# Attention and quantised feed-forward on one core: other units for VectorE, down weights turned in their own tile, eight row buffers and biases spread by a product

## The reference

```python
xn = layernorm(x)                                   # over 1024, no affine
# attention: for each row, its 32 heads attend to each other (D = 32)
q, k, v = (xn @ Wq.T + bq), (xn @ Wk.T + bk), (xn @ Wv.T + bv)     # -> (B, S, 32, 32)
s = einsum('bshd,bsgd->bshg', q, k) / sqrt(32)
s = where(s > 0.001, s, -inf)
o = einsum('bshg,bsgd->bshd', softmax(s), v).reshape(B, S, 1024)
attn = o @ Wo.T + bo
# feed-forward, inner width 3584
Wg, Wu, Wd = dequant(gate_q, gate_s), dequant(up_q, up_s), dequant(down_q, down_s)
ffn = (silu(xn @ Wg.T) * (xn @ Wu.T)) @ Wd.T
out = x + attn + ffn
```

## Time and profile before

| | |
|---|---|
| median of 3 runs | 2102.8 us (2102.1 to 2103.78) |
| the profiled execution | 2104.22 us, span from first to last instruction 2102.2 us |
| opening, to the first scores | 0 to 79.5 us |
| attention and output projection | to about 857 us |
| feed-forward tiles 0 and 1, few or no downs yet | to 935 us |
| feed-forward tiles 2 to 26 | 935 to 2005 us |
| tile 27 | 2005 to 2047 us |
| tail | 2047 to 2102.2 us |
| TensorE, VectorE, ScalarE, GpSimd busy | 96%, 76%, 60%, 64% |

### The profile page before, as it was taken

One profiled execution on the slowest core, in us unless ns is written; L12 is line 12 of the kernel. 1 busy time (PEld: TensorE's weight loads), 2 busy tenths in 40 slices (PEclk: granted clock), 3 DMA queues, 4 the chain that ended last, 5 costly groups with the idle time before them and its releaser, 6 DMA issues. The chain is left out here.

```text
span 2102.2 us, 36938 instructions
## 1 busy us (share of the span) xinstructions
PE 2017.6 (96%) x10880; PEld 972.4 (46%) x10880; DVE 1592.0 (76%) x1584; ACT 1252.8 (60%) x2017; POOL 1349.7 (64%) x769
## 2 busy tenths in 40 slices
PE   7899999999998899899999999999999999999997
PEld 5555555555554444334444444444444444444444
DVE  5666766667665300599899989999899989998996
ACT  4578778777775311255666566665656566656653
POOL 1445554645543000058888888888888888888886
PEclk9999999999999999999999999999999999999999
DMA  8363553554454352122122212222112212221208
GB/s 290 91 132 88 106 133 85 113 121 90 111 109 130 101 195 97 30 70 61 45 50 70 60 45 50 53 63 59 48 46 70 60 45 50 68 55 51 50 22 324
DMA packets 330006, 185.97 MB, mean 88 GB/s; under 512 B 269168, under 2 KB 306032, under 8 KB 329968
## 3 DMA queue, kind: packets, MB, share of 16 engines
q1 hardware_dynamic: 329968, 185.46, 34.0%
HBM read 96.29 MB, written 25.17 MB: 58 GB/s over the span
## 5 line engine op out<-in xcount | busy, mean ns | idle before, releaser
L644 PE MATMUL banks<-xt,lower 128*128 128x512 f16 x3584 | 861.7, 379 | 30.0 <-ACT lower L895 16.3
L1212 POOL TENSOR_TENSOR acc<-acc,lower 128x1024 f32<-128x1024 f32 x327 | 772.8, 2368 | 175.2 <-ACT lower L922 175.2
L922 ACT ACTIVATE lower<-banks,down_scale 128x512 f32<-128x512 f32 x654 | 413.8, 683 | 355.9 <-PE banks L669 264.0
L1099 DVE SCALAR_TENSOR_TENSOR lower<-banks,gate_scale,lower 128x1024 f32<-128x1024 f32 x392 | 479.2, 1278 | 146.2 <-PE banks L644 140.2
L644 PEld LDWEIGHTS banks<-xt,lower 128*128 128x128 f16 x3584 | 337.4, 98 | 486.6 <-DVE lower L1099 80.2
L499 PE MATMUL banks<-wt,xt_tile 128*128 128x512 f16 x2304 | 540.0, 380 | 4.2 <-ACT wt L743 2.6
L1099 DVE SCALAR_TENSOR_TENSOR lower<-banks,up_scale,lower 128x1024 f32<-128x1024 f32 x392 | 479.5, 1278 | 51.1 <-PE banks L644 44.9
L669 PE MATMUL banks<-lower 128*128 (+1 forms) x1792 | 458.8, 380 | 5.0 <-DMA lower<-lower 4.4
L1174 POOL TENSOR_TENSOR stacks<-unit,stacks 128x512 f16<-128x512 f32 x192 | 246.7, 1308 | 286.6 <-ACT stacks L768 286.5
L499 PEld LDWEIGHTS banks<-wt,xt_tile 128*128 (+1 forms) x2304 | 215.8, 98 | 220.6 <-issue 4.7
L669 PEld LDWEIGHTS banks<-lower 128*128 (+1 forms) x1792 | 175.2, 98 | 217.6 <-issue 17.3
(11 more groups left out here) (57 smaller groups left out, 1305.8 us busy)
## 6 DMA issues: line engine op xcount, KB each, us to landing
lower<-in_L_ffn_gate_q_dram SPq DMA_DIRECT2D x28, 512.0 KB, 3.7
lower<-in_L_ffn_up_q_dram SPq DMA_DIRECT2D x28, 512.0 KB, 4.5
lower<-in_L_ffn_down_q_dram SPq DMA_DIRECT2D x28, 512.0 KB, 4.1
x_tile<-in_L_attn_x_dram SPq DMA_DIRECT2D x16, 512.0 KB, 3.8
xt_scratch<-xt_tile SPq DMA_DIRECT2D x16, 512.0 KB, 2.8
ctx_scratch<-ctx_parts SPq DMA_DIRECT2D x64, 128.0 KB, 2.1
lower<-ctx_scratch SPq DMA_DIRECT2D x4, 2048.0 KB, 9.2
xt<-xt_scratch SPq DMA_DIRECT2D x4, 2048.0 KB, 15.4
```

What stands on the lines that cost most here:

```text
L644: last = mm(psum[:, 2 * (slot % 3) + c, :], gu_t[:, mat, g, :], xt[:, (2 * half + c) * CT:(2 * half + c + 1) * CT, part, g, :], start=(par ...
L922: run(down_tmp[:, buffer, c * BANK:(c + 1) * BANK], psum[:, 6 + c, :], ACT.Copy, scale=scale)\
L1099: v.scalar_tensor_tensor(out=acc_of[:, half, :], in0=gu_pair(slot % 3), scalar=scale[:, :, :].rearrange("p t k -> p (t k)")[:, bass.ds(t * ...
L1212: g.tensor_tensor(acc[:, half, ho, :], acc[:, half, ho, :], down_tmp[:, buffer, :], ALU.add).then_inc(down_added, 1)
```

## The change

Feed-forward:

- The fast downs are `d` 0, 2, 8 and 10, at units 16, 20, 0 and 4 (`d % 8 in (0, 2)`); there are still 4 of 16.
- GpSimd's `hidden` for half 1 comes after unit 7 and no longer after unit 10. ScalarE's second SiLU comes at unit 27 and no longer at 23.
- The down weights of tile `t` are converted in tile `t` (after unit 25) and turned behind it, no longer in tile `t + 1`. Gate is converted after unit 9 (was 21), up after unit 29 (was 27).
- In the tail ScalarE's conversion of the last down weights is gone, and its two HI parts stand ahead of its second and fourth copies, no longer ahead of all copies.

Opening:

- `w_rows` holds eight blocks (`ROWS = 8`), so blocks are loaded up to eight ahead, and the quarters begin at `w = 8` (eight of them come after the last block).
- The three bias rows are loaded to one partition each. TensorE multiplies a column of ones with them (two float32 products of 512 columns for each row), and ScalarE copies the result to `bias_qkv`, ahead of everything but its first square root. The blocks `w` 1 and 2 wait for all three copies.
- The second row tile is normed in steps at `w` 10 to 13 and turned behind the load of block 21. `bo` is loaded last.

```diff
-                w_rows = sb(s1, "w_rows", [P, 4, H], F32)
+                w_rows = sb(s1, "w_rows", [P, ROWS, H], F32)
...
-            for w in range(4, 3 * KT):
-                weights(w)
-                quarter(w - 4)
-                if w == NEXT_NORM:
-                    next_norm()
-                if w == NEXT_NORM + 2:
-                    next_x()
-            for s in range(3 * KT - 4, 3 * KT):
+            for w in range(ROWS, 3 * KT):
+                weights(w)
+                quarter(w - ROWS)
+                second_x(w)
+            for s in range(3 * KT - ROWS, 3 * KT):
                 quarter(s)
...
-            return d % 4 == 0
+            return d % 8 in (0, 2)
...
-        CONV_DOWN, CONV_GATE, CONV_UP = 7, 21, 27
+        CONV_GATE, CONV_DOWN, CONV_UP = 9, 25, 29
         HI_AT0, HI_AT1 = 3, 13
-        POOL_AT = {0: ("h", 0), 4: ("l", 0), 10: ("h", 1), 18: ("l", 1)}
+        SILU_AT = {19: 0, 27: 1}
+        POOL_AT = {0: ("h", 0), 4: ("l", 0), 7: ("h", 1), 18: ("l", 1)}
...
+                if w in (1, 2):
+                    pe.wait_ge(bias_ready, 3)
...
+            def spread_bias(n):
+                pe.wait_ge(bias_loaded[n], 16)
+                for c in range(2):
+                    last = mm(bias_pair(n)[:, c * BANK:(c + 1) * BANK], ones[:], bias_rows[n][:, c * BANK:(c + 1) * BANK],
+                              start=True, stop=True)
+                last.then_inc(bias_spread, 1)
...
+            def bias_out(n):
+                act.wait_ge(bias_spread, n + 1)
+                ...
+                run(dst, src, ACT.Copy).then_inc(bias_ready, 1)
...
-            conv(DOWN, NI - 1)
-            hidden_hi(NI - 1, 0)
-            hidden_hi(NI - 1, 1)
             for n, (t, d) in enumerate(TAIL_POOL):
+                if n in (1, 3):
+                    hidden_hi(NI - 1, n // 2)
                 down_copy(t, d, TAIL_FROM + n)
...
-            for w in range(4):
+            for n, b in enumerate((bq, bk, bv)):
+                sp.dma_start(bias_rows[n], b.rearrange("(a n) -> a n", a=1)).then_inc(bias_loaded[n], 16)
+            for w in range(ROWS):
                 load_w(w)
             turn_x(0)
-            for w in range(4, 8):
-                load_w(w)
-            for dst, b in ((bias_qkv[:, 0, :], bq), (bias_qkv[:, 1, :], bk),
-                           (unit32[:, :, :].rearrange("p a n -> p (a n)"), bv)):
-                sp.dma_start(dst, b.rearrange("(a n) -> a n", a=1).broadcast_to((P, H))).then_inc(bias_loaded, 16)
...
                 load_q(UP, t + 1)
-                if has_prev(t):
-                    turn_q(DOWN, t - 1)
-                    load_q(DOWN, t)
                 turn_q(GATE, t + 1)
+                turn_q(DOWN, t)
+                load_q(DOWN, t + 1)
                 turn_q(UP, t + 1)
```

More of the change, by code:

```diff
@@ L59, in build @@
     W_SCALE = 64.0
+    ROWS = 8
     W_UNSCALE = 1.0 / W_SCALE
@@ L144, in build @@
         const_ready = sem("const_ready")
-        w_loaded = [sem(f"w_loaded{k}") for k in range(4)]
+        w_loaded = [sem(f"w_loaded{k}") for k in range(ROWS)]
         w_turned = sem("w_turned")
@@ L148, in build @@
         w_lo = sem("w_lo")
-        bias_loaded = sem("bias_loaded")
-        bias_turned = sem("bias_turned")
+        bias_loaded = [sem(f"bias_loaded{k}") for k in range(4)]
+        bias_spread = sem("bias_spread")
+        bias_ready = sem("bias_ready")
         x_loaded = sem("x_loaded")
@@ L376, in by_dve @@
         def by_dve(d):
-            return d % 4 == 0
+            return d % 8 in (0, 2)
         def slow_rank(d):
-            return d - d // 4 - 1
+            return sum(not by_dve(e) for e in range(d))
         SLOTS = []
@@ L386, in build @@
             SLOTS.append(("gu", unit))
-            if unit % 8 == 0:
+            if unit % 16 in (0, 4):
                 SLOTS.append(("down", unit))
@@ L609, in tile_2 @@
                             head_products(i - 1, n)
+            def spread_bias(n):
[4 more added lines that the diff above has]
+                last.then_inc(bias_spread, 1)
             def first_tile():
-                opening(weights, lambda: None, first_quarter, lambda: None, lambda: None)
+                for n in (Q, K, V):
+                    spread_bias(n)
+                opening(weights, lambda: None, first_quarter, lambda w: None)
                 for m in range(4):
```

91 lines of the change are left out of this document (54 added, 37 removed).

## The result

The changed kernel takes 2087.88 us (median of 6 runs, 2086.79 to 2088.61) where the kernel before took 2102.45 us in the same comparison (6 runs, 2101.71 to 2103.78): a ratio of 0.993, 95% interval 0.9917 to 0.9943. That is 14.6 us less. The forecast was 26.5 us less; the direction and the range hold, the size does not. The profiled execution has a span of 2086.5 us against 2102.2.

What follows compares the result with a forecast made beforehand. TensorE was taken to bound the kernel, busy 96% of the span, leaving mostly its pauses to win. Feed-forward -21.5, opening -6 and tail +1 sum to -26.5 us: 2102.8 to 2076.3 us, range 2067 to 2090.

Steps and rivals of the forecast that it cites:

- Feed-forward, forecast -21.5: Feed-forward, tiles 2 to 27: GpSimd's earlier product ends ScalarE's HI wait; 0.85 us for each of 25 tiles, -21.5 us in all.
- one rival: Feed-forward: the stall only moves, GpSimd's five adds holding the slow banks for the 0.8 us saved; 2095 us, chance 0.10.
- just fits: Feed-forward: ScalarE's copy for unit 12 waits 0.7 us, its halves done at 18.9 and 19.5, wanted at 19.3 and 19.7.
- The rival of the slower clump: Feed-forward: three VectorE adds in a row cost TensorE 1.0 us at units 6 and 22, not 0.24; 2115 us, chance 0.05.
- Opening, forecast -6: Opening: the last quarters end at 68 us instead of 74.0, -6 us; bounds -9 and -2.
- I take 7 us: Opening: six float32 bias products take 7 us, TensorE reaching full clock on the way; spreading ends near 11.5 us.
- The rival that the opening gives nothing: Opening: dear products, block 8 late and TensorE at half clock; 2082.3 us, chance 0.14.
- The spread of the biases over 10 us: Opening: spreading the biases for over 10 us was listed among the signs that the prediction is wrong.
- just covered: Opening: block 8, asked for at 17.5 us behind the row tile's turning, is there at 22, in time.
- Tail, forecast +1: Tail: TensorE's 4.41 us wait and half clock vanish, but the second LO part and later adds come 1.2 us later; +1 us.
- bound of +3: Tail: the bad end of the forecast, +3 us, if TensorE runs at half clock again after its new pauses.
- The rival that the tail was bound by its wait: Tail: TensorE's wait for down weights was the bound, so all 6 us come back; 2069 us, chance 0.08.

## Why the prediction was right, and where it was wrong

**Feed-forward, forecast -21.5, measured -21.0.** The mechanism holds step by step. `hidden` for half 1 begins at 987.12, 13.4 us into its tile (forecast 13.5), the HI part starts without a wait, and ScalarE is free as unit 16 is made. The tile is 41.97 us (forecast 41.9), with the pauses of 0.24 us behind units 4 and 20. The stall did move, as one rival had it, but to a place where it is covered: ScalarE's copy for unit 12 waits 0.94 us for its buffer, where I had worked out 0.7, and begins 18.4 us into the tile (forecast 18.2). TensorE found its banks free but for 0.05 us, which is the "just fits" of the forecast. The run with unit 10 put back shows that this one wait carries it. The rival of the slower clump did not come: VectorE was idle when unit 3 was ready (979.17, 0.30 us), and TensorE lost 0.24 us to the three adds in a row, not 1.0.

**Opening, forecast -6, measured -2.8 (3.4 by the medians of the run that undoes it).** The pace behind block 8 was right to 0.1 us (45.1 against 34.7 + 10.3). The term that failed is "I take 7 us" for the six products: they took 10.5, a little over the upper bound of 10.2 that stood there. The step that led me off was the clock: I let it rise 4.6 us after TensorE's first work, as it does in the trace of before with transpositions over 128 rows, and here the rows from 4.00 to 14.51 stand at half rate to their end. Of the rule cited there, four passes for true FP32 (the Trainium skill, FP8 and Floating Point Precision, TensorE Precision Notes): the trace agrees at both clocks, 1.71 us and 0.86 us for 512 columns against 0.43 and 0.216 for float16. The rival that the opening gives nothing had the same dear products, and counted half clock behind block 8, which did not come. The spread of the biases over 10 us was named as a sign of being wrong, and it was that. The second term, block 8 asked for at 17.5 and "just covered", moved with the first: the row tile was turned behind the products, block 8 was asked for at 21.05, 3.5 us later than forecast, and was turned 4.8 us after that (forecast 4.6 to its arrival) with a pause of 0.20 us. "Just covered" was right for this kernel, and wrong as a general picture: the run without the products shows that the issue of a turning in front of it can take 6.24 us.

**Tail, forecast +1, measured +8.1.** The chain that I wrote down is the chain in the trace: five downs ahead, a pause before the sixth, the second HI part behind the third copy, VectorE's second LO part behind that. The sizes of its first terms were wrong. I set the products at 3.28 us and the first LO part at 1.2, as in before. There, GpSimd had nothing to add from 2049.49 to 2055.83. TensorE, which waited for the down weights, made the first slow down of the tail only then: ScalarE was done with its conversion and HI parts at 2052.80 and still waited 1.44 us for that down. GpSimd's and ScalarE's timelines of before, which I had not set beside the earlier trace rows:

```profile
2047.14 2.35 POOL L1212 TENSOR_TENSOR acc<-acc,lower 128x1024 f32<-128x1024 f32 x1 [0.23 <-ACT lower L922]
2055.83 7.98 POOL L1212 TENSOR_TENSOR acc<-acc,lower 128x1024 f32<-128x1024 f32 x3 [6.33 <-ACT lower L922]
...
2054.24 1.51 ACT L922 ACTIVATE lower<-banks,down_scale 128x512 f32<-128x512 f32 x2 [1.44 <-PE banks L669]
```

The change takes TensorE's wait away, so that five downs are made at once, and it puts copies ahead of the HI parts. Both together feed GpSimd, which adds all through: products 5.65 us, LO part 3.36, together 4.5 us more. (With the HI parts first GpSimd stays quiet for 4.54 us, although the down weights are there early in that run too.) Counted from the last unit, the 7.1 us over the forecast come like this. The sixth down begins at 11.6 us and not at 7.4, 4.2 late. VectorE's second LO part ends at 19.2 and not at 13.6, 5.6 late: the downs between went at half clock, and the LO part took 2.5 us and not 2.2. The last 1.5 us come behind it, where TensorE works at half rate again until 2047.5. The forecast had allowed for this half clock only in its bound. The rule that I cited for the second LO part (the Trainium skill, GPSIMD Engine Reference, Specifications: GpSimd shares its SBUF interfaces with VectorE and contends with instructions of two SBUF inputs) names what slowed these rows, and the trace agrees (2.52 us for that LO part, and 3.49 us for the products instead of 5.65 when GpSimd is held); I applied it to one of four instructions of that kind. The bound of +3 was too narrow because it took VectorE's rows of before as given, although the edit moved the work that ran beside them. The rival that the tail was bound by its wait is out: in the run with the HI parts first TensorE's wait for weights is gone, a pause of 3.87 us for ScalarE stands near its place, and the tail is 54.9 us against 55.4. The wait stood beside work on the other engines that takes as long.

Sum: -2.8 - 21.0 + 8.1 = -15.7 us of span, as the traces have it, against -21.5 - 6 + 1.

That the total stayed in the range of 2067 to 2090 is in part luck. The feed-forward, four fifths of the forecast, was right for the reasons given, and it carries the direction. But the tail alone missed its bound of +3 by 5 us, and the total is held because the range had room for three bad ends at once (2102.8 - 15 - 2 + 3 = 2088.8). No rival described what happened; the one nearest in time, 2082.3, had the opening giving nothing and the tail as forecast.

## What to carry to other kernels

When an edit moves work on one engine, list what it will now feed, and whether that runs beside instructions of another engine whose length was read while it was quiet: a duration from a trace holds only with its neighbours. A pause removed from TensorE is worth little if the engine behind it is late anyway: here the tail without it took 54.9 us against 55.4 at best, and 63.5 where the work let through early ran beside the engine that was late. The new pauses cost their length and then a stretch of half clock (7.1 and 4.8 us, then TensorE at 0.5 until 2037.3 and 2047.5). Behind a queue of loads, put what is urgent ahead of a transfer that turns, and check in SyncE's rows how long its issue takes.

## What the runs showed of the hardware

**VectorE and GpSimd take turns.** In the tails of these kernels each VectorE instruction with two SBUF inputs that begins while GpSimd adds ends about 1.09 us after GpSimd's instruction, whatever its own start. The rows of single instructions in the changed kernel's tail, VectorE's first product, and the third of GpSimd's adds:

```profile
2024.38 2.35 DVE L1148 TENSOR_TENSOR lower<-lower 128x1024 f32<-128x1024 f32 x1
```

```profile
2029.06 3.17 POOL L1250 TENSOR_TENSOR acc<-acc,lower 128x1024 f32<-128x1024 f32 x1
```

GpSimd's adds end at 2025.65, 2028.94, 2032.23 and 2041.10; VectorE's four instructions end at 2026.73, 2030.03, 2033.31 and 2042.18, 1.08 or 1.09 later each. The kernel before has it too: its first product, which begins at 2048.43 beside the add that ends at 2049.49, ends at 2050.58. GpSimd's own next adds in the changed kernel are 3.05 and 3.17 us long and not 2.35. VectorE's adds from PSUM, with one SBUF input, stay at 1.2 us beside GpSimd (ten in 12.09 us in the tile above).

**The issue of a turning transfer lasts until the loads ahead of it are worked off**: 1.87 us (four loads ahead), 2.93 (six), 6.24 (eight), all asked for at about 9.7 us, and 12.50 us for the second one behind all loads. It is what is still under way that counts, not the number asked for. In the windows view the loads of the run with eight move 393 GB/s until 14 us and 247 in the next one, and the issue ends at 15.87; with six it is 401 GB/s until 11 us, then 228, and the issue ends at 12.56. In the kernel before (10 to 11 us) and in the changed one (15 to 19) nothing moves, and the issue takes 1.87 and 2.14 us, in the changed one with eight loads asked for ahead of it. Loads are not all that sets it: K's turning, another shape, takes 4.7 to 5.6 us in these traces.

**Float32 products over one row did not raise TensorE's clock from 1.2 GHz**: 10.5 us of them without a pause stood at the half rate to their end, while the same products over 128 rows ended at the full rate (one run, from 8.8 us on, 4.1 us after their start). Five traces have the one-row products (the changed kernel, and the runs with unit 10, with the HI parts first, with the HI part one copy earlier and with GpSimd held). In all five the products last from about 4 to 14.5 us, and full rate comes at 17.7 to 20.6 us, 3.2 to 6.1 us after the first transposition. In the five traces without them the transpositions from 5.4 to 5.6 us on bring it at 10.1 to 11.7. Which property of the rows it is (zeros in the other 127 count here as rows) was not tried.
